# A binarised 3x3 convolution on one core: M added by VectorE from the fifth weight load on, and the first products placed between the last loads' sums

## The reference

```python
# x: (64, 256, 28, 28); M: (256, 256, 3, 3); Z: (8, 256, 256, 3, 3); alpha: (256, 1, 1); rv: (1, 8)
g  = x.reshape(B, 32, 8, H, W)                       # group norm, 32 groups, eps 1e-5
xn = ((g - mean(g)) / sqrt(var(g) + 1e-5)).reshape(x.shape)

A   = m*m + sum(z*z, axis=0) / 100                   # m = M flat, z = Z flat, 8 draws
inv = rsqrt(A)
w   = rv @ (z * inv) + m * inv                       # = (rv @ z + m) * inv
bw  = sign(w).reshape(M.shape)
ba  = sign(xn)
out = x + conv2d(ba, bw, stride 1, padding 1) * alpha
```

## Time and profile before

| | |
|---|---|
| median of 3 runs | 480.31 us |
| the profiled execution | 480.06 us |
| its span (what the trace covers) | 478.3 us |
| PE busy | 451.8 us, 94% |
| DVE busy | 397.0 us, 83% |
| ACT busy | 326.1 us, 68% |
| HBM traffic | 259 GB/s over the span |
| chain that ended last | PE 80%, ACT 5%, SPq 4%, DVE 4%, DMA 3% |

### The profile page before, as it was taken

One profiled execution on the slowest core, in us unless ns is written; L12 is line 12 of the kernel. 1 busy time (PEld: TensorE's weight loads), 2 busy tenths in 40 slices (PEclk: granted clock), 3 DMA queues, 4 the chain that ended last, 5 costly groups with the idle time before them and its releaser, 6 DMA issues.

```text
span 478.3 us, 8267 instructions
## 1 busy us (share of the span) xinstructions
PE 451.8 (94%) x2966; PEld 424.5 (89%) x2966; DVE 397.0 (83%) x781; ACT 326.1 (68%) x564; POOL 10.8 (2%) x55
## 2 busy tenths in 40 slices
PE   3778898999999999999999999999999999999994
PEld 1333467999999999999999999999999999999994
DVE  2468687899989898989898989899898989898686
ACT  2556887785959494949494959586777768594420
POOL 3000000000000000000000000000000000000000
PEclk9979999999999999999999999999999999999998
DMA  7999999078777777777776776767766677632345
GB/s 268 399 394 391 392 356 393 13 259 325 259 259 253 252 268 271 269 271 269 264 274 222 270 263 253 252 235 275 257 259 254 250 252 252 250 120 117 134 182 223
DMA packets 46234, 124.55 MB, mean 260 GB/s; under 512 B 3696, under 2 KB 4208, under 8 KB 46192
## 3 DMA queue, kind: packets, MB, share of 16 engines
q1 hardware_dynamic: 45488, 123.21, 70.4%
q10 hardware_dynamic: 704, 0.81, 0.5%
HBM read 72.62 MB, written 51.38 MB: 259 GB/s over the span
## 4 chain that ended last, share of the span: by engine, by line
PE 80%; ACT 5%; SPq 4%; DVE 4%; DMA 3%; issue 2%; DVEq 0%; ACTq 0%
PE conv_ps L402 76%; SPq L283 4%; DMA x_sb<-in_L_conv_Z_dram 2%; ACT signs L550 2%; PE wt_ps L360 2%; PE conv_ps L340 1%; DVE low L856 1%; DVE whole L847 1%; DMA part<-in_L_conv_M_dram 1%; DVE x_sb L875 1%; ACT unread L531 1%; ACT unread L533 1%; ACT whole L498 1%; SPq L286 1%; PE conv_ps L347 1%
## 5 line engine op out<-in xcount | busy, mean ns | idle before, releaser
L402 PE MATMUL conv_ps<-signs,wts 128*128 128x378 f32 (+3 forms) x2304 | 403.9, 337 | 3.1 <-ACT part L564 2.2
L402 PEld LDWEIGHTS conv_ps<-signs,wts 128*128 128x128 f32 x2304 | 401.1, 189 | 6.3 <-ACT part L564 3.3
L550 ACT ACTIVATE signs<-x_sb,shift,rstd 128x784 fp32r<-128x784 f32 x128 | 133.7, 1099 | 21.3 <-DVE shift L833 21.3
L564 ACT ACTIVATE part<-conv_ps 128x392 int32<-128x392 f32 x128 | 62.4, 487 | 68.3 <-PE conv_ps L402 68.3
L847 DVE SCALAR_TENSOR_TENSOR whole<-conv_ps,part 128x392 int32<-128x392 f32 x128 | 72.2, 564 | 38.5 <-PE conv_ps L402 34.9
L856 DVE SCALAR_TENSOR_TENSOR low<-whole,conv_ps 128x392 f32<-128x392 int16 x128 | 71.9, 562 | 4.4
L777 DVE BATCH_NORM_STATS2 bn<-x_sb 128x6 f32<-128x392 f32 x138 | 70.6, 556 | 0.0
L875 DVE SCALAR_TENSOR_TENSOR x_sb<-whole,alpha_sb,x_sb 128x1568 f32<-128x1568 int16 (+1 forms) x38 | 60.6, 1594 | 0.8
L875 DVE SCALAR_TENSOR_TENSOR x_sb<-low,alpha_sb,x_sb 128x1568 f32<-128x1568 f32 (+1 forms) x38 | 60.4, 1588 | 0.0
L533 ACT ACTIVATE unread<-x_sb 128x784 bf16<-128x784 f32 x59 | 50.4, 854 | 0.0
L531 ACT ACTIVATE unread<-x_sb 128x784 bf16<-128x784 f32 x59 | 50.2, 851 | 0.0
(11 more groups left out here) (56 smaller groups left out, 118.1 us busy)
## 6 DMA issues: line engine op xcount, KB each, us to landing
x_sb<-in_x_dram SPq DMA_DIRECT2D x64, 784.0 KB, 5.0
out_dram<-x_sb SPq DMA_DIRECT2D x62, 784.0 KB, 4.8
x_sb<-in_L_conv_Z_dram SPq DMA_DIRECT2D x64, 288.0 KB, 9.0
part<-in_L_conv_M_dram SPq DMA_DIRECT2D x8, 288.0 KB, 10.1
out_dram<-x_sb SPq DMA_DIRECT2D x1, 588.0 KB, 3.9
out_dram<-x_sb ACTq DMA_DIRECT2D x1, 588.0 KB, 4.5
out_dram<-x_sb SPq DMA_DIRECT2D x2, 98.0 KB, 3.2
out_dram<-x_sb ACTq DMA_DIRECT2D x2, 98.0 KB, 3.5
```

Of the source, the lines that this page charges most:

```text
L402: mm = pe.matmul(flat_tile(conv_ps[at][:, 0:COLUMNS], b, r0, r1, c0, c1), wts[:, ch, (down + 1) * KW + right + 1], e, start=n == 0, stop=n ...
L550: nc.scalar.activation(o, x_sb[:, slot_of(k * TRI + image), h], ACT.Sign, bias=shift[:, k % RING, image, h:h + 1], scale=rstd[:, k % RING, ...
L564: nc.scalar.activation(part[:, at, 0:COLUMNS], conv_ps[at][:, 0:COLUMNS], ACT.Copy, scale=-FRACTION / PACK, bias=FRACTION / 2).then_inc(pa ...
```

## The change

M is added by PE in loads 0 to 3 and by DVE from load 4 on. The banks of the q sums are given out so that banks 2 and 3 are free for products from load 6 on; the SP waits for DVE's addition before it overwrites M's buffer. All 36 products of the first half of the input channels for the four tiles of pair one come before the packing of the second half: 9, 4, 6, 6, 4 and 7 of them. The first pair's scale, shift and signs move from load 5 to load 4. Both DVE copies of the first half's weights stand in load 5. After the loads, image 2 is done by DVE alone, the statistics of image 4 come behind tile 1, `bounded` and `negative_mean` come ahead of tile 0's `low_sum`, and ACT does `fraction` 2 ahead of the four signs of the second pair.

```diff
-    M_LOADS = LOADS - 2
-    EARLY = 5
-    THIRD = 2
+    M_LOADS = LOADS // 2
+
+    EARLY = (TAPS, 4, 6, 6, 4, 7)
+    assert sum(EARLY) == TOPS * TAPS
...
-        taps_ps = [conv_ps[1], conv_ps[0], conv_ps[1], conv_ps[3], wt_ps[1], wt_ps[2]]
+        taps_ps = [conv_ps[1], conv_ps[0], conv_ps[2], wt_ps[0], wt_ps[1], wt_ps[2]]
+        def q_bank(unit):
+            return unit % 4 if unit < UNITS - 4 else 2 + unit % 2
...
-        ALONE = (0, 1, 4, 5, 9)
+        ALONE = (0, 1, 2, 4, 5, 9)
...
@@ SP, load_weights
+                need(sp, m_added, 2 * (c - ZR + 1 - M_LOADS))
...
@@ PE, q_sums
-                        need(pe, w_done, unit - 3)
+                        if c < LOADS - 2:
+                            need(pe, w_done, unit - 3)
+                        else:
+                            pe.wait_ge(m_added, unit - 1 - 2 * M_LOADS)
...
@@ PE
+            def early_products(i):
+                for n in range(sum(EARLY[:i]), sum(EARLY[:i + 1])):
+                    b, place = divmod(n, TAPS)
+                    products(0, b, bank(b), place, place + 1)
...
             for c in range(LOADS):
                 q_sums(c, 0)
+                if c == BUILD_AT + 1:
+                    pack_early(2)
                 if c == LOADS - 2:
-                    pe.wait_ge(dve_wts_done, 1)
-                    pe.wait_ge(act_wts_done, 1)
-                    pe.wait_ge(signs_done, PAIR)
-                    products(0, 0, bank(0), 0, 2 * KW)
+                    early_products(1)
                 if c == LOADS - 1:
-                    products(0, 1, bank(1), 0, EARLY)
+                    early_products(4)
                 a_sums(c, 0)
                 q_sums(c, 1)
                 if c == LOADS - 2:
-                    pe.wait_ge(dve_wts_done, 2)
-                    products(0, 0, bank(0), 2 * KW, TAPS)
+                    early_products(2)
                 a_sums(c, 1)
                 if c == BUILD_AT:
                     pack_early(0)
                     pack_early(1)
-                if c == BUILD_AT + 1:
-                    pack_early(2)
-            products(0, 1, bank(1), EARLY, TAPS)
-            pe.wait_ge(w_done, DONE_EARLY)
-            products(0, 2, bank(2), 0, THIRD)
+                if c == LOADS - 3:
+                    pe.wait_ge(dve_wts_done, 2)
+                    pe.wait_ge(act_wts_done, 1)
+                    pe.wait_ge(signs_done, PAIR)
+                    early_products(0)
+                if c == LOADS - 2:
+                    early_products(3)
+            early_products(5)
+            pe.wait_ge(m_added, UNITS - 2 * M_LOADS)
...
@@ after the packing of the second half
-            products(0, 2, bank(2), THIRD, TAPS)
...
-                first_products(0, b, b, TAPS if b == 2 else 0)
+                first_products(0, b, b, TAPS if b < TOPS else 0)
...
@@ ACT, in the loads
+                if c == LOADS - 4:
+                    deviation(0, 0, 0, PAIR)
                 if c >= 1:
                     unit_sign(2 * c - 2)
                     unit_sign(2 * c - 1)
-                if c == LOADS - 3:
-                    deviation(0, 0, 0, PAIR)
+                if c == LOADS - 4:
                     half_signs(0, 0, 0)
                     half_signs(0, 0, 1)
...
@@ ACT, after the loads
-            sums(2)
             fraction(0, 0)
             sums(3)
             fraction(1, 1)
+            fraction(2, 2)
             deviation(1, 0, PAIR, TRI)
-            half_signs(1, 0, 4)
-            half_signs(1, 0, 5)
-            fraction(2, 2)
-            half_signs(1, 0, 6)
-            half_signs(1, 0, 7)
+            for n in range(HALVES * PAIR, HALVES * TRI):
+                half_signs(1, 0, n)
             fraction(3, 3)
...
@@ DVE, in the loads
-                    unit_w(2 * c - 2)
-                    unit_w(2 * c - 1)
+                    for u in range(2 * c - 2, 2 * c):
+                        if c - 1 >= M_LOADS:
+                            unit_w_of_sum(u)
+                        else:
+                            unit_w(u)
                 if c == BUILD_AT + 1:
                     copy_taps(0)
-                if c == BUILD_AT + 2:
                     copy_taps(2)
                 part_squares(c, 1)
...
                 if c == LOADS - 4:
                     bounded(0, 0, 0, PAIR)
+                    negative_mean(0, 0, 0, PAIR)
                 unit_a_sum(2 * c)
                 unit_a_sum(2 * c + 1)
-                if c == LOADS - 3:
-                    negative_mean(0, 0, 0, PAIR)
...
@@ DVE, after the loads
             image_stats(3)
+            group_steps(1, 0, TRI)
+            high_sum(0, 0, 0)
+            bounded(1, 0, PAIR, TRI)
+            negative_mean(1, 0, PAIR, TRI)
+            low_sum(0, 0, 0)
+            tile_sums(0, 1)
             image_stats(4)
-            group_steps(1, 0, TRI)
-            tile_sums(0, 0)
-            bounded(1, 0, PAIR, TRI)
-            tile_sums(0, 1)
-            negative_mean(1, 0, PAIR, TRI)
             image_stats(5, lambda: tile_sums(0, 2))
```

More of the change, by code:

```diff
@@ L337, in q_sums @@
                     if p == 0:
-                        need(pe, w_done, unit - 3)
+                        if c < LOADS - 2:
+                            need(pe, w_done, unit - 3)
+                        else:
+                            pe.wait_ge(m_added, unit - 1 - 2 * M_LOADS)
                     for j in range(KQ):
-                        mm = pe.matmul(q_ps[unit % 4][j * QUAD:(j + 1) * QUAD, 0:CW], mix[:, p],
+                        mm = pe.matmul(q_ps[q_bank(unit)][j * QUAD:(j + 1) * QUAD, 0:CW], mix[:, p],
                                        z_sb[:, c % ZR, p, j, cols], start=p == 0, stop=p == 1)
@@ L346, in q_sums @@
                         for j in range(KQ):
-                            pe.matmul(q_ps[(2 * c + u) % 4][j * QUAD:(j + 1) * QUAD, 0:CW],
+                            pe.matmul(q_ps[q_bank(2 * c + u)][j * QUAD:(j + 1) * QUAD, 0:CW],
                                       one[:, j * QUAD:(j + 1) * QUAD], m_sb[:, c % ZR, u * CW:(u + 1) * CW],
@@ L386, in pack_early @@
                 if n == 2:
-                    pe.wait_ge(dve_wts_done, 1)
+                    pe.wait_ge(m_added, 2)
                 pack(n, 0)
@@ L738, in unit_w @@
                 need(dve, w_sign_done, c - QR + 1)
-                nc.vector.tensor_tensor(w[:, c % QR], q_ps[c % 4][:, 0:CW], inv[:, c % QR],
+                nc.vector.tensor_tensor(w[:, c % QR], q_ps[q_bank(c)][:, 0:CW], inv[:, c % QR],
                                         ALU.mult).then_inc(w_done, 1)
@@ L745, in unit_m @@
                 dve.wait_ge(q_done, c + 1)
-                dve.wait_ge(w_sign_done, c - QR + 1)
-                nc.vector.tensor_tensor(w[:, c % QR], q_ps[c % 4][:, 0:CW],
+                need(dve, w_sign_done, c - QR + 1)
+                nc.vector.tensor_tensor(w[:, c % QR], q_ps[q_bank(c)][:, 0:CW],
                                         m_sb[:, c // 2 % ZR, c % 2 * CW:(c % 2 + 1) * CW], ALU.add
```

## The result

The changed kernel took 481.5 us (median of 11 runs, 481.12 to 482.09), the kernel before 479.96 us (11 runs, 478.73 to 480.69): ratio 1.0036, 95% interval 1.0025 to 1.0047. It is 1.5 us slower; forecast were 1.5 us. The profiled execution has a span of 480.4 us, 2.1 more than before; about 0.6 of that is not the change's but of this execution, the slowest of the eleven (482.09), whose weights landed later. In e5 and in the runs of the kernel before that go with e5 to e8 one execution each (628.0 and 630.7 us, at a granted clock of 0.66) is in the number of runs and not in the ratio; without it e5's median is 479.87.

A forecast was written before the change was run, and what follows sets the result against it. The prediction took DVE's shift of set 1 (90.70 us) to set the end. Its terms, +0.7, +1.0, -0.6 and +0.4, made +1.5 us: 481.8 us by the median, range 479.9 to 483.1 (480.8 to 482.6 by the parts' bounds).

The forecast's parts named there:

- What sets the end: Whole kernel: whatever moves DVE's shift of set 1 (90.70 us) moves the end by the same amount.
- Rival B: From 80.49 to 126 us PE's count decides; 9 products done earlier save 1.6 us, giving 478.7; chance 0.10.
- Part 1: Loads 4 and 5: sooner first signs, M additions and copies on DVE put `a_sums(5,1)` at 52.85, not 52.17; +0.7 us.
- Part 2: PE's queue from `a_sums(5,1)` to `a_sums(7,1)`: 14.4 us without a wait, last sum 1.7 later, +1.0 beyond the first signs' delay.
- Rival A: Loads: smaller PE backlog, from ACT's freedom in load 6 or cheaper weight changes, leaves half of 1.7; 480.9; chance 0.14.
- The price of a group: PE in the loads: each group of products between sums costs another 0.30 us for the change to and fro.
- Part 3: From the last sum to ACT's sum of image 3: +1.1 in place of 1.7, so -0.6 us; `group_steps(1)` at 75.9.
- Its term of 0.14: After the last sum: PE waits an estimated 0.14 us for the weights before five products of tile 0.
- Part 4: From `group_steps(1)` to the shift of set 1: 15.87 - 2.7 + 2.6 + 0.5 = 16.3 us, +0.4.
- PE would wait more than 0.37 us for ACT in front of 127.8: Sign of a right forecast: PE's wait for ACT before its final unbroken run of products exceeds 0.37 us.
- The stall near 93 to 95: PE stalls about 2 us there as ACT's `fraction` 6 is 1.5 late; a second clock fall after it costs nothing.
- Rival C: PE's clock falls in the loads after pauses, costing 0.9 to 1.5 us, giving 482.7 to 483.3; chance 0.08.

The follow-up runs named there:

- e5: Changed kernel with DVE's statistics of image 4 back ahead of `group_steps(1)`; 479.96 us, ratio 1.0001 to the kernel before.
- e8: Changed kernel with `fraction` 6 moved ahead of ACT's root and first two signs of set 1; 481.38 us, ratio 1.0034 to the kernel before.
- e1: Changed kernel with only its part in the loads, the order after the loads being that of the kernel before; 482.05 us, ratio 1.0053 to the kernel before.
- e6: Changed kernel's loads, 33 early products in fewer groups, then the kernel before's order with `fraction` 2 ahead of the four signs; 478.96 us, ratio 0.9977.
- e7: e6 with the statistics of image 9 shared, one channel half on ACT; 477.83 us, ratio 0.9958 to the kernel before.
- e9: e4 with the statistics of image 9 shared, one half on ACT behind `fraction` 9; 477.53 us, ratio 0.9962 to the kernel before.
- e2: Kernel before with only the new order after the loads, loads and early products unchanged; 480.22 us, ratio 1.0010 to the kernel before.
- e3: Changed kernel with its 29 products ahead of the last squares sum in three groups, not five; 480.75 us, ratio 1.0022 to the kernel before.
- e4: Kernel before with one line moved, `fraction` 2 ahead of the second pair's four signs; 477.98 us, ratio 0.9965 to the kernel before.

## Why the prediction was right

**What sets the end** was right: shift of set 1 +2.13, last product +2.13. The distance between the two was 380.74 us in both kernels and 380.70 to 380.78 in e1 to e6 and e8. Only e7 and e9, which take work out between the shifts of set 1 and set 2, have another (380.10). Rival B (PE's count) fell, most plainly in e2: three us ahead at product 82 and 0.5 later at the end. e8 shows the same for a stall taken away. The count is not far off, though: e9 meets it once the shift of set 2 comes 1.1 sooner.

**Part 1**, first signs and copies ahead of `a_sums(5,1)`: +0.7 forecast. The changed kernel's own trace has +1.38, with its 0.6 of late weights in it; e1, with the same loads and weights on time, has 52.81, +0.64. No run separates the sooner signs from the later additions of M; that part rests on the rows.

**Part 2**, PE's queue: 14.4 us forecast from there to the last sum, 14.57 measured (14.55 in e1), against 13.43 before. Without a wait, as said. Rival A fell with it. The price of a group, 0.30, was a little low: 0.36 by e3, and 0.33 on average over all five (14.57 + 0.06, less 12.96 for the blocks and the products themselves, makes 1.67).

**Part 3**: -0.6 forecast; from the last sum to `group_steps(1)` 9.23 became 8.49, -0.74. Its term of 0.14 for PE's wait for the copied weights had no row behind it; the wait was 0.45.

**Part 4**: 15.87 became 16.22, +0.35 for +0.4 forecast, and e5 shows that its one large term, image 4, is there. Together 0.64 + 1.12 - 0.74 + 0.35 = 1.4 us, and 1.5 were measured. So the sum came out part by part and not because errors cancelled. Whether it would show as slower was nearly even in my numbers (0.45 to 0.44), and the 1.5 stand just over the 1.44 that I took for the bound: that side of it is luck.

**What was off.** I wrote that PE would wait more than 0.37 us for ACT in front of 127.8. It did not wait there. The stall near 93 to 95 came (2.2 us), the clock did fall behind it (0.66 over 95 to 100, 17 products), and PE lost all the room it had before product 316, so that it and `fraction` 16 arrived together. e3 has the same order and the same stall, its clock stayed up, and there PE did wait, 0.39 at 113.38 and 0.55 at 126.80. PE's timeline of e3, then the same stretch in e3 and in the changed kernel:

```profile
93.88 18.41 PE L411 MATMUL conv_ps<-signs,wts 128*128 128x378 f32 x104 [2.23 <-ACT part L577]
```

```profile
95.00:100.00 5.00, 5.00 (x31) 5.00 (x30) 4.83 (x15) 5.00 (x9) 0.00 (x0) 1.00 0.87 321
```

```profile
95.00:100.00 5.00, 4.45 (x17) 4.45 (x18) 4.90 (x10) 5.00 (x8) 0.00 (x0) 0.66 0.52 204
```

That the fall costs nothing was right (e8, e3), but only just. A fall behind the stall at 80, which the working left open, did not come in this execution. Rival C did not show: the granted clock was 1.00 from 50 to 80 us. Ahead of that it was lower for a while (0.83 over 30 to 40, in the kernel before 0.98), but that is load 3, where the two kernels are the same, and e1 with the same loads had 0.96. The condition that I gave C, a pause of about 1.84 us, is not a sure sign either: e3's 2.23 passed without a fall. The profile pair alone would have said 2.1 us and not 1.5: a span holds the DMA's luck too.

## What to carry to other kernels

Before you move work forward into an engine's idle time, ask whether the engine's own queue still reaches its next critical instruction in time, and whether this engine is the one that is late at the end. Here the moved products made PE late for the weights and early for everything else. Find the one event that the end follows (here a VectorE instruction some 380 us ahead of it), and price each edit by what it does to that event; e7 and e9 show where this stops, as soon as the work behind the event changes. An instruction that stands behind others that wait for something it doesn't need is the cheap gain: one moved line gave 0.35%.

## What the runs showed of the hardware

A change to and fro between the short 32-column sums and full products costs PE 0.30 to 0.36 us (e3), about two products.

Early work can lengthen a later stall, and the granted clock can fall with it: PE idled 3.38 us in e1 and 1.86 in e6 and ran at half clock behind it in both (0.51 over 82 to 85, 9 products; 0.71, 14 products), but not behind 0.8 us in e4 (1.00, 17 products) nor behind 1.24 in the changed kernel at 80.84. The length of the stall alone doesn't decide it. The clock fell behind 2.23 us in the changed kernel (at 95.55) and stayed at 1.00 behind 2.23 in e3 (at 93.88) and 2.18 in e2 (at 93.95).

What a fall costs hangs on where it lies. In e1 and e6 it lay on products that DVE waited for, and the 1.0 us that e6 lost this way was more than its six further products were worth. In e5 (2.11 us of stall, 0.55 over 82 to 85) DVE waited for no product, and nothing was lost.

In the kernel before the fall lies ahead of products that DVE waited for too (0.39 and 0.57 us, the second and third wait of the earlier trace rows), and its executions differ with their clock. Of the 23 that go with e1 to e4, 11 had a mean granted clock of 0.990 or more and a median of 479.28 us, 12 had 0.988 or less and 480.23. Its profile (0.985) is one of the second kind. All six executions of e4 had 0.990 or more, so of its 1.95 us some 1.3 stay against the first group, and the rest may be the fall that no longer comes. This split is not shown by a trace: the runs give the mean clock of an execution and not where it fell.
